# A graph attention kernel: the left sides of its sort by matmul, built in wide VectorE operations or column by column

## The chip, the cores and the metric

One core of a Trainium2 chip runs the kernel in one launch. The time is the device time of that core in microseconds: 1287.59 us is the median of three executions (1286.08, 1287.59 and 4121.88), and the profiled execution took 1285.94 us.

## The reference

A graph layer on 6250 nodes (rows of x, 96 values) and 106,250 edges (src, dst). It computes, cut to what matters:

```
q = (x[src] @ qW), k = (x[dst] @ kW), v = (x[dst] @ vW)      # 4 heads of 24
w = exp(clip(sum over a head of q * k, -10, 10))
res[n] = sum over edges with src = n of (w / (sum of w of the node + 1e-8)) * v
out = layernorm(x + (x + res)), over the 96 values
```

The edges come sorted by dst. The kernel needs them grouped by src, so that a tile of 128 edges has all its sources in one block of 128 nodes.

## The kernel before

**Start.** TensorE projects the nodes; q stays in on-chip memory (`qt`), k and v of all nodes go to a table in device memory (`kv_dram`).

**Sort.** The edges lie as 125 partitions x 850 columns. The columns fall into six groups of 140, 110, 130, 160, 160 and 150. For each group VectorE ranks the edges (`mark`, `pair`, `count`, `base`, `select`, `tree`, `own_position`), which gives every edge its row in a tile (`pos_p`, 0 to 127) and a tile number plus a half (`pos_t`). Then the edges are moved by matmuls, ten columns at a time, called a unit: there are 85 units, 14 of them in group 0. For each column j of a unit TensorE multiplies a left side `lhs[:, q] = (q == pos_p) * payload` (125 partitions x 128) with a right side `theta[:, t]`, a step over the tile numbers, and adds all of a group's products up in `ps_a` and `ps_b`, one for each half of the payload (`pay_a`, `pay_b`). So a unit is 20 matmuls (L620).

- VectorE, `unit`: one comparison over all ten columns at once gives the one-hot tile `lhs_1` (L1037, 125 x 1280 in f16: a ramp `iota_s`, repeated for ten columns, against `pos_p` broadcast over 128 places); two multiplications (L1041, L1044) give `lhs_a` and `lhs_b` with the payloads, broadcast in the same manner. `between(i)` places one of the iteration's own additions (L1103) behind each of the first two.
- ScalarE, `unit`: the steps `theta`, one operation for each column (L707). In group 0 VectorE makes the first four of a unit's ten steps in one operation (L1033, 125 x 744).
- Left and right sides are double buffered by `vm`: a unit waits until TensorE is through with the unit before the last (`s_bin`).

After a group's last unit `differ`, `turn`, `choice` and `pick` turn the sums into the row numbers `dst_s` for the gathers.

**Iterations.** Then 176 iterations of five tiles each: GpSimd gathers the k and v rows of 128 edges with one indirect DMA for each tile (L499, five to a batch, 171 batches, eight buffers); TensorE fetches q by a one-hot matmul (L636), VectorE multiplies q and k (L1122), weighs v (L1132), sums over heads (L1142), adds the results of five tiles to the accumulators (L1103), builds the one-hot tiles of a later iteration (L1111) and clips (L1150); ScalarE takes the exponential and copies; TensorE sums up per node (L650).

**The order** is written out by hand in `plan()`. Group 0 is ranked and sorted before the iterations begin (`sort_stretch`, where VectorE's and the other engines' units run in a loop of two). The ranking and the units of group g (1 to 5) lie within the iterations that use group g-1: first iterations with pieces of the ranking, then iterations with one or two units each; `pick` of group g comes 3 or 4 iterations before the group's first tile. In an iteration VectorE does, in this order, L1122, L1132, an addition, L1142, an addition, L1111, L1150, an addition, and then the unit with the last two additions in it. TensorE does a unit one iteration later than VectorE.

GpSimd issues batch n once VectorE and TensorE are through with a batch some iterations back (6 in the first five groups, 8 buffers in the last), and the first batch of a group once the group is sorted (`s_sorted`, which `pick` signals).

Of the kernel before, what the change touches and what calls it, by code (L numbers as in the profile page):

```python
# [5 lines left out]
def gnn(nc, x, src, dst, qW, kW, vW, out):  # L6
    f32, i32, u16 = mybir.dt.float32, mybir.dt.int32, mybir.dt.uint16
    f16, bf16 = mybir.dt.float16, mybir.dt.bfloat16
    ALU = mybir.AluOpType
    ACT = mybir.ActivationFunctionType  # L10
    AX = mybir.AxisListType

    P = 128
# [6 lines left out]
    EP, EC = 125, E // 125  # L20
# [4 lines left out]
    SU = 10  # L25
    KD = 4
# [4 lines left out]
    GC = [140, 110, 130, 160, 160, 150]  # L31
# [36 lines left out]
    CMAX, TMAX = max(GC), max(TS)  # L68
# [81 lines left out]
    with ExitStack() as ctx:  # L150
        def sb(name, shape, dt):
            return ctx.enter_context(nc.sbuf_tensor(name, shape, dt))
# [4 lines left out]
        def sem(name):  # L157
            return ctx.enter_context(nc.semaphore(name))
# [1 line left out]

        iota_i = sb("iota_i", [P, IW], i32)
        iota_f = sb("iota_f", [P, IW], f32)
        iota_s = sb("iota_s", [P, P, SU], f16)
        pos_h = sb("pos_h", [EP, GC[0]], f16)
        iota_u = sb("iota_u", [P, NB], u16)
        part_i = sb("part_i", [P, 1], i32)
        part_f = sb("part_f", [P, 1], f32)
# [18 lines left out]
        dst_i = sb("dst_i", [EP, EC], i32)  # L186
        tmp_i = sb("tmp_i", [EP, CMAX], i32)
        bin_u = sb("bin_u", [EP, CMAX], u16)
        pay_a = sb("pay_a", [EP, EC], f16)
        pay_b = sb("pay_b", [EP, EC], f16)  # L190
        pos_p = sb("pos_p", [EP, EC], f16)
        pos_t = sb("pos_t", [EP, EC], f32)

        rank_u = sb("rank_u", [EP, CMAX], u16)
        same_u = sb("same_u", [EP, CMAX], u16)
        steps_m = sb("steps_m", [P, max(NB * CMAX, 2 * NPC * PC * D)], f16)
        place_m = sb("place_m", [EP, max(14 * CMAX, 6 * P * SU)], u16)
        kst_m = sb("kst_m", [EP, NB * (KMAX + 2)], f16)
        kb_m = sb("kb_m", [EP, NB * (KMAX + 2)], u16)
        cnt_f = sb("cnt_f", [EP, NB], f32)  # L200
# [29 lines left out]


        LW = P * SU
        lhs_m = place_m[:, 0:6 * LW].bitcast(f16)
        lhs_1 = lhs_m[:, 0:2 * LW].rearrange("p (i q c) -> p i q c", i=2, c=SU)
        lhs_a = lhs_m[:, 2 * LW:4 * LW].rearrange("p (i q c) -> p i q c", i=2, c=SU)
        lhs_b = lhs_m[:, 4 * LW:6 * LW].rearrange("p (i q c) -> p i q c", i=2, c=SU)
        theta = steps_m[0:EP, 0:2 * SU * (TMAX + 1)].rearrange("p (i c t) -> p i c t", i=2, c=SU)
        cum_a = sb("cum_a", [P, max(TMAX + 1, max(GT))], f32)
        cum_b = sb("cum_b", [P, TMAX + 1], f32)
# [9 lines left out]
        ohb = sb("ohb", [P, 4, P, U], bf16)  # L249
        onehT = sb("onehT", [P, 2, U * P], f32)  # L250
        oneh = sb("oneh", [P, 2, U, P], f32)
        T1 = TS[0] + 1
        iota_d = oneh[:, :, :, :].rearrange("p i u n -> p (i u n)").bitcast(f16)[:, 0:T1 * KD]
        iota_d = iota_d.rearrange("p (t c) -> p t c", c=KD)
        theta_d = onehT[0:EP, :, :].rearrange("p i n -> p (i n)").bitcast(f16)[:, 0:2 * T1 * KD]
        theta_d = theta_d.rearrange("p (i t c) -> p i t c", i=2, c=KD)
        prod = sb("prod", [P, 2, U * D], f32)
        score = sb("score", [P, 2, U * HEADS], f32)
        clipped = sb("clipped", [P, 2, U * HEADS], f32)
# [66 lines left out]
        s_lhs_a = sem("s_lhs_a")  # L326
        s_lhs = sem("s_lhs")
        s_half = sem("s_half")
        s_one_lhs = sem("s_one_lhs")
        s_theta = sem("s_theta")  # L330
        s_bin = sem("s_bin")
        s_dif = sem("s_dif")
# [60 lines left out]
        def sort_stretch(eng, unit, g, v0, v1):  # L393

            if not unit:
                return
            a = min(v1, v0 + 2)
            b = a + max(0, v1 - 1 - a) // 2 * 2
            for v in range(v0, a):
                unit(g, v, v % 2)  # L400
            if b > a:
                with eng.Fori(a, b - 1, 2) as i:
                    for k in range(2):
                        unit(g, i + k, (a + k) % 2)
            for v in range(b, v1):
                unit(g, v, v % 2)

        def there(n):
# [105 lines left out]
        def _(pe):  # L514
# [94 lines left out]
            def unit(g, v, vm):  # L609
                w = TS[g] + 1  # L610
                first = isinstance(v, int) and v == V0[g]
                last = isinstance(v, int) and v == V0[g + 1] - 1
                if first:
                    pe.wait_ge(s_blk, g + 1)
                pe.wait_ge(s_theta, v + 1)
                for ps, lhs, s_made in ((ps_a, lhs_a, s_lhs_a), (ps_b, lhs_b, s_lhs)):
                    pe.wait_ge(s_made, v + 1)
                    for j in range(SU):
                        steps = theta_d[:, vm, :, j] if g == 0 and j < KD else theta[:, vm, j, 0:w]
                        mm = nc.tensor.matmul(ps[:, 0:w], lhs[:, vm, :, j], steps,  # L620
                                              start=first and j == 0, stop=last and j == SU - 1)
                    if last and ps is ps_a:
                        mm.then_inc(s_half, 1)
                mm.then_inc(s_bin, 1)

            def tiles(m, mm, sorts):
# [38 lines left out]
                for sort in sorts:  # L665
                    unit(*sort)
# [5 lines left out]
        @block.scalar  # L672
        def _(act):
            act.wait_ge(s_ramp, 1)
            nc.scalar.activation(iota_s[:, :, :], iota_f[:, 0:P].unsqueeze(2).to_broadcast([P, P, SU]), ACT.Copy)
            nc.scalar.activation(iota_d, iota_f[:, 0:T1].unsqueeze(2).to_broadcast([P, T1, KD]), ACT.Copy)
            nc.scalar.activation(iota_t[:, :, :], iota_f[:, 1:P + 1].unsqueeze(2).to_broadcast([P, P, U]),
                                 ACT.Copy).then_inc(s_wide, 1)

# [96 lines left out]
            for j, (a, b) in enumerate(PARTS):  # L776
                act.wait_ge(s_inv, j + 1)
                for i in range(a, min(b, NPC - 1)):
                    for k in range(PC if i < NPC - 2 else HALF):
                        if j + 1 < len(PARTS) and i == b - 1 and k == (PC - 2 if b < NPC - 2 else 2):  # L780
                            root(j + 1)
                        n = i * PC + k
                        last = nc.scalar.activation(yout[i][:, k, :], acc[:, n, 0:D], ACT.Identity,
                                                    scale=inv[:, n:n + 1], bias=shift[:, n:n + 1])
# [4 lines left out]
        def _(dve):  # L789
            own = [0]  # L790

            def link(ins):

                own[0] += 1
                ins.then_inc(s_own, 1)
                dve.wait_ge(s_own, own[0])
# [212 lines left out]
            def own_position(g):  # L1009

                C, _, pl, _, _ = group_views(g)
                c0, c1 = C0[g], C0[g + 1]
                t, s = tmp_i[:, 0:C], src_i[:, c0:c1]
                link(nc.vector.tensor_tensor(t, pl[:, 0, :], rank_u[:, 0:C], ALU.add))
                link(nc.vector.scalar_tensor_tensor(s, t, P - 1, flip[:, 0:C], ALU.bitwise_and, ALU.bitwise_xor))
                link(nc.vector.tensor_copy(pos_p[:, c0:c1], s))
                link(nc.vector.tensor_scalar(t, t, 7, None, ALU.logical_shift_right))
                if g == 0:
                    link(nc.vector.tensor_scalar(pos_h[:, :], t, 0.5, None, ALU.add))
                nc.vector.tensor_scalar(pos_t[:, c0:c1], t, 0.5, None, ALU.add).then_inc(s_pos, 1)  # L1020
                dve.wait_ge(s_pos, g + 1)

            def unit(g, v, vm, between=lambda i: None):
                if isinstance(v, int) and v == 0:
                    dve.wait_ge(s_wide, 1)
                wait(dve, s_bin, v - 1)
                cols = bass.ds(v * SU, SU)

                def spread(a):
                    return a[:, cols].unsqueeze(1).to_broadcast([EP, P, SU])  # L1030

                if g == 0:
                    nc.vector.tensor_tensor(theta_d[:, vm, :, :], iota_d[0:EP, :, :],  # L1033
                                            pos_h[:, cols].unsqueeze(1).to_broadcast([EP, T1, SU])[:, :, 0:KD],
                                            ALU.is_le)
                wait(dve, s_lhs, v - 1)
                nc.vector.tensor_tensor(lhs_1[:, vm, :, :], iota_s[0:EP, :, :], spread(pos_p),  # L1037
                                        ALU.is_equal).then_inc(s_one_lhs, 1)
                between(0)
                dve.wait_ge(s_one_lhs, v + 1)  # L1040
                nc.vector.tensor_tensor(lhs_a[:, vm, :, :], lhs_1[:, vm, :, :], spread(pay_a),  # L1041
                                        ALU.mult).then_inc(s_lhs_a, 1)
                between(1)
                nc.vector.tensor_tensor(lhs_b[:, vm, :, :], lhs_1[:, vm, :, :], spread(pay_b),  # L1044
                                        ALU.mult).then_inc(s_lhs, 1)

            def differ(g):

# [197 lines left out]
            for k in range(HALF, PC):  # L1246
                n = (NPC - 2) * PC + k
                last = nc.vector.tensor_scalar(yout[NPC - 2][:, k, :], acc[:, n, 0:D], inv[:, n:n + 1],
                                               shift[:, n:n + 1], ALU.mult, ALU.add)
            last.then_inc(s_ylast, 1)  # L1250
            n = (NPC - 1) * PC
# [31 lines left out]
```

## Time and profile before

| | |
|---|---|
| median of three runs | 1287.59 us |
| profiled execution | 1285.94 us |
| its span, first to last instruction | 1284.1 us |
| VectorE (DVE) busy | 1030.2 us, 80% |
| TensorE (PE) busy | 988.8 us, 77% |
| GpSimd (POOL) busy | 912.9 us, 71% |
| ScalarE (ACT) busy | 660.6 us, 51% |
| TensorE clock, mean granted | 0.734 |

Busy times are the union of an engine's instructions; instructions of VectorE overlap at their ends, so that the time from start to start of two in a row is shorter than the duration of one. Idle time is put down to what ended it. The clock is given as a share of full speed, 2.4 GHz.

### The profile page before, as it was taken

Reading aid. Unit: us, or ns where it says so; the run is one execution under the profiler, and the core shown is the slowest. Engines: PE = TensorE matmul, PEld = TensorE weight load, DVE = VectorE, ACT = ScalarE, POOL = GpSimd, SP = SyncE. Lnnn points to the kernel's source line nnn. Section 1 sums busy time; section 2 is a strip of 40 time slices with the busy share of each in tenths; the row PEclk is TensorE's granted clock in tenths of the full one; section 3 lists DMA queues with packets and bytes.
Section 4 is the critical chain, followed back from the end, with each engine's and each line's share of the span. In section 5 each row is a group of like instructions: output and inputs, shape, how many; then the busy total and the mean of one; then the engine's idle time right before and its main releaser. Section 6 shows DMA issues by size and latency. Waiting matters only on the chain.

```text
span 1284.1 us, 23009 instructions
## 1 busy us (share of the span) xinstructions
PE 988.8 (77%) x6512; PEld 897.6 (70%) x6513; DVE 1030.2 (80%) x3048; ACT 660.6 (51%) x1469; POOL 912.9 (71%) x887
## 2 busy tenths in 40 slices
PE   8876878678866887867987877878877688888870
PEld 6765776577856887756886766767767677777760
DVE  8999997899889999889987779977768755555557
ACT  6842792259622799223997332587624322222225
POOL 1217787777777777777777777777777777777752
PEclk9986796669875799776898775688859955555555
DMA  6202222222222222222222222222252222222222
GB/s 173 84 13 76 73 66 78 74 69 69 73 79 67 71 71 70 81 75 75 69 69 70 74 73 74 72 71 70 73 150 78 79 80 77 79 78 79 77 62 75
DMA packets 67241, 98.34 MB, mean 77 GB/s; under 512 B 33127, under 2 KB 53204, under 8 KB 67134
## 3 DMA queue, kind: packets, MB, share of 16 engines
q0 software_dynamic: 41040, 84.10, 24.1%
q1 hardware_dynamic: 26094, 12.94, 3.9%
q8 instruction: 51, 0.84, 0.3%
q14 instruction: 56, 0.46, 0.1%
HBM read 89.77 MB, written 7.22 MB: 76 GB/s over the span
## 4 chain that ended last, share of the span: by engine, by line
POOL 27%; DVE 25%; issue 15%; ACT 14%; PE 12%; DVEq 3%; DMA 2%; SPq 0%; POOLq 0%; ACTq 0%
POOL kv L499 27%; ACT steps_m L707 10%; DVE acc L1103 5%; PE ps_r L650 3%; PE ps_q L636 2%; DVE prod L1122 2%; ACT oneh L758 2%; DMA kv<-kv_table,dst_s 2%; DVEq L414 2%; DVE place_m L997 2%; DVE steps_m L834 2%; DVE place_m L1001 2%; PE ps_a L620 1%; ACT onehT L752 1%; PE ps_b L620 1%
## 5 line engine op out<-in xcount | busy, mean ns | idle before, releaser
L499 POOL DMA_INDIRECT kv<-kv_table,dst_s x855 | 890.0, 1041 | 305.3 <-issue 298.9
L636 PE MATMUL ps_q<-qt,onehT 128*128 x1760 | 322.3, 348 | 103.7 <-ACT onehT L752 91.0
L650 PE MATMUL ps_r<-wv,oneh 128*128 128x100 f32 x1752 | 329.9, 356 | 91.7 <-DVE wv L1132 91.4
L636 PEld LDWEIGHTS ps_q<-qt,onehT 128*128 128x128 f32 x1760 | 293.0, 255 | 131.2 <-issue 130.7
L650 PEld LDWEIGHTS ps_r<-wv,oneh 128*128 128x128 f32 x1752 | 301.7, 263 | 109.5 <-DVE wv L1132 105.7
L707 ACT ACTIVATE steps_m<-iota_f,pos_t 125x254 f16<-125x254 f32 (+4 forms) x794 | 311.8, 490 | 17.4 <-PE ps_b L620 10.2
L1103 DVE TENSOR_TENSOR acc<-acc,ps_r 128x100 f32 x876 | 221.2, 252 | 60.2 <-issue 23.7
L1122 DVE TENSOR_TENSOR prod<-ps_q,kv 128x480 f32<-128x480 f32 x176 | 115.0, 653 | 144.1 <-DMA kv<-kv_table,dst_s 138.5
L745 ACT ACTIVATE wv<-clipped 128x20 f32<-128x20 f32 x176 | 38.6, 219 | 360.0 <-DVE clipped L1150 359.8
L752 ACT ACTIVATE onehT<-ps_t 128x640 f32<-128x640 bf16 x176 | 123.7, 703 | 182.6 <-PE ps_t L662 176.6
L758 ACT ACTIVATE oneh<-ohb 128x640 f32<-128x640 bf16 x176 | 163.1, 927 | 1.3 <-PE ps_r L650 1.3
L620 PE MATMUL ps_a<-steps_m,place_m 125*128 125x254 f16 (+4 forms) x794 | 107.7, 287 | 26.8 <-ACT steps_m L707 26.8
L1132 DVE TENSOR_TENSOR wv<-kv,wv 128x480 f32<-128x480 f32 x176 | 114.1, 648 | 2.9 <-issue 2.2
L1142 DVE TENSOR_REDUCE score<-prod 128x20 f32<-128x480 f32 x176 | 113.5, 645 | 0.5
L620 PEld LDWEIGHTS ps_a<-steps_m,place_m 125*128 125x128 f16 x794 | 88.0, 142 | 35.0 <-ACT steps_m L707 29.0
L662 PE MATMUL ps_t<-ident_bf,ohb 128*128 128x128 bf16 x880 | 103.9, 266 | 9.6 <-DVE ohb L1111 9.1
L620 PE MATMUL ps_b<-steps_m,place_m 125*128 125x254 f16 (+4 forms) x794 | 101.8, 277 | 0.0
L662 PEld LDWEIGHTS ps_t<-ident_bf,ohb 128*128 128x128 bf16 x880 | 90.3, 139 | 15.0 <-DVE ohb L1111 13.6
L1111 DVE TENSOR_TENSOR ohb<-iota_t,loc_s 128x640 bf16<-128x640 bf16 x176 | 98.1, 557 | 0.0
L620 PEld LDWEIGHTS ps_b<-steps_m,place_m 125*128 125x128 f16 x794 | 89.7, 141 | 4.1
L1037 DVE TENSOR_TENSOR place_m<-iota_s,pos_p 125x1280 f16<-125x1280 f16 x85 | 69.6, 819 | 6.5 <-PE ps_b L620 6.5
L1041 DVE TENSOR_TENSOR place_m<-place_m,pay_a 125x1280 f16<-125x1280 f16 x85 | 69.6, 819 | 1.6
(204 smaller groups left out, 655.0 us busy)
## 6 DMA issues: line engine op xcount, KB each, us to landing
kv<-kv_table,dst_s POOLq DMA_INDIRECT x855
kv_table<-kv SPq DMA_DIRECT2D x7, 672.0 KB, 3.7
acc<-in_x_dram SPq DMA_DIRECT2D x6, 336.0 KB, 8.1
steps_m<-in_x_dram SPq DMA_DIRECT2D x6, 336.0 KB, 6.6
out_dram<-kv SPq DMA_DIRECT2D x6, 336.0 KB
dst_i<-in_dst_dram SPq DMA_DIRECT2D x1, 415.0 KB
src_i<-in_src_dram SPq DMA_DIRECT2D x1, 346.7 KB
acc<-in_x_dram SPq DMA_DIRECT2D x1, 288.0 KB, 4.5
```

The lines of the kernel that those rows point to most:

```text
L499: nc.gpsimd.indirect_dma_start(kv[:, nm, u, :], None, kv_dram, bass.IndirectOffsetOnAxis(ap=dst_s[:, n * U + u:n * U + u + 1], axis=0)).th ...
L620: mm = nc.tensor.matmul(ps[:, 0:w], lhs[:, vm, :, j], steps, start=first and j == 0, stop=last and j == SU - 1)
L636: last = nc.tensor.matmul(ps_q[nm % 2][:, u * D:(u + 1) * D], onehT[:, nm % 2, u * P:(u + 1) * P], qt[:, bass.ds(blks[u], 1), :].rearrange ...
L650: last = nc.tensor.matmul(to, oneh[:, nm % 2, u, :], wv[:, nm % 2, u, :], start=True, stop=True)
L662: last = nc.tensor.transpose(ps_t[nm % 2][:, u * P // 2:(u + 1) * P // 2].bitcast(bf16), ohb[:, nm % 4, :, u], ident_bf[:, :])
L707: last = nc.scalar.activation(theta[:, vm, j, 0:w], iota_f[0:EP, 0:w], ACT.Sign, scale=-1.0, bias=pos_t[:, bass.ds(v * SU + j, 1)])
L752: nc.scalar.activation(onehT[:, nm % 2, :], ps_t[nm % 2][:, 0:U * P // 2].bitcast(bf16), ACT.Copy).then_inc(s_oneT, 1)
L758: nc.scalar.activation(oneh[:, nm % 2, :, :], ohb[:, nm % 4, :, :].rearrange("p n u -> p u n"), ACT.Copy).then_inc(s_onf, 1)
L1103: nc.vector.tensor_tensor(at, at, from_ps, ALU.add).then_inc(s_acc, 1)
L1122: nc.vector.tensor_tensor(prod[:, nm % 2, :].rearrange("p (u d) -> p u d", u=U), ps_q[nm % 2][:, 0:U * D].rearrange("p (u d) -> p u d", u= ...
L1132: nc.vector.tensor_tensor(wv[:, nm % 2, :, 0:D].rearrange("p u (h d) -> p u h d", h=HEADS), kv[:, km, :, D:2 * D].rearrange("p u (h d) -> ...
L1142: nc.vector.tensor_reduce(score[:, nm % 2, :], prod[:, nm % 2, :].rearrange("p (h d) -> p h d", d=DH), axis=AX.X, op=ALU.add).then_inc(s_s ...
```

## The change

The unit's left sides are made column by column. Each column j of each half is one tensor_scalar of 128 columns: the ramp `iota_h` (f16) is compared with the edge's place `pos_p[:, c]` and multiplied with its payload `pay[:, c]`, both read as one value for each partition. That is 20 operations for a unit where there were three, and `lhs_1` and its semaphore go. `pos_p`, `pay_a` and `pay_b` become f32. The layout of the left sides turns from (place, column) to (column, place), so a matmul reads 128 values in a row. `between(0)` now stands behind the fifth operation and `between(1)` behind the tenth.

In group 0 VectorE's four steps of a unit are four tensor_scalar operations of 186 columns with `pos_t[:, c]` as the scalar, into the same `theta` tile that ScalarE fills; `theta_d`, `iota_d` and `pos_h` go. Units of group 0 are written out one by one on all engines instead of in a loop of two, since a scalar's column is fixed in the instruction.

```
-            nc.scalar.activation(iota_s[:, :, :], iota_f[:, 0:P].unsqueeze(2).to_broadcast([P, P, SU]), ACT.Copy)
-            nc.scalar.activation(iota_d, iota_f[:, 0:T1].unsqueeze(2).to_broadcast([P, T1, KD]), ACT.Copy)
+            nc.scalar.activation(iota_h[:, :], iota_f[:, 0:max(P, TS[0] + 1)], ACT.Copy)
...
-                if g == 0:
-                    link(nc.vector.tensor_scalar(pos_h[:, :], t, 0.5, None, ALU.add))
...
-                        steps = theta_d[:, vm, :, j] if g == 0 and j < KD else theta[:, vm, j, 0:w]
-                        mm = nc.tensor.matmul(ps[:, 0:w], lhs[:, vm, :, j], steps,
+                        mm = nc.tensor.matmul(ps[:, 0:w], lhs[:, vm, j, :], theta[:, vm, j, 0:w],
...
                 if g == 0:
-                    nc.vector.tensor_tensor(theta_d[:, vm, :, :], iota_d[0:EP, :, :],
-                                            pos_h[:, cols].unsqueeze(1).to_broadcast([EP, T1, SU])[:, :, 0:KD],
-                                            ALU.is_le)
-                wait(dve, s_lhs, v - 1)
-                nc.vector.tensor_tensor(lhs_1[:, vm, :, :], iota_s[0:EP, :, :], spread(pos_p),
-                                        ALU.is_equal).then_inc(s_one_lhs, 1)
+                    w = TS[0] + 1
+                    for j in range(KD):
+                        nc.vector.tensor_scalar(theta[:, vm, j, 0:w], iota_h[0:EP, 0:w], pos_t[:, c0 + j:c0 + j + 1],
+                                                None, ALU.is_le)
+
+                def left(to, pay, a, b):
+                    for j in range(a, b):
+                        c = c0 + j
+                        last = nc.vector.tensor_scalar(to[:, vm, j, :], iota_h[0:EP, 0:P], pos_p[:, c:c + 1],
+                                                       pay[:, c:c + 1], ALU.is_equal, ALU.mult)
+                    return last
+
+                left(lhs_a, pay_a, 0, SU // 2)
                 between(0)
-                dve.wait_ge(s_one_lhs, v + 1)
-                nc.vector.tensor_tensor(lhs_a[:, vm, :, :], lhs_1[:, vm, :, :], spread(pay_a),
-                                        ALU.mult).then_inc(s_lhs_a, 1)
+                left(lhs_a, pay_a, SU // 2, SU).then_inc(s_lhs_a, 1)
                 between(1)
-                nc.vector.tensor_tensor(lhs_b[:, vm, :, :], lhs_1[:, vm, :, :], spread(pay_b),
-                                        ALU.mult).then_inc(s_lhs, 1)
+                left(lhs_b, pay_b, 0, SU).then_inc(s_lhs, 1)
```

## Rows read from the trace of the kernel before

**Rows 1.** The page, its first section: busy us (share of the span) xinstructions of each engine.

```profile
PE 988.8 (77%) x6512; PEld 897.6 (70%) x6513; DVE 1030.2 (80%) x3048; ACT 660.6 (51%) x1469; POOL 912.9 (71%) x887
```

**Rows 2.** Timeline, VectorE, an iteration with one unit: start us, us, engine, line, operation.

```profile
429.39 0.64 DVE L1122 TENSOR_TENSOR prod<-ps_q,kv 128x480 f32<-128x480 f32 x1
...
432.14 0.81 DVE L1037 TENSOR_TENSOR place_m<-iota_s,pos_p 125x1280 f16<-125x1280 f16 x1
432.88 0.24 DVE L1103 TENSOR_TENSOR acc<-acc,ps_r 128x100 f32 x1
433.04 0.81 DVE L1041 TENSOR_TENSOR place_m<-place_m,pay_a 125x1280 f16<-125x1280 f16 x1
...
433.95 0.81 DVE L1044 TENSOR_TENSOR place_m<-place_m,pay_b 125x1280 f16<-125x1280 f16 x1
434.68 0.64 DVE L1122 TENSOR_TENSOR prod<-ps_q,kv 128x480 f32<-128x480 f32 x1
```

**Rows 3.** Timeline, VectorE, first operation of the first sort and the one behind it.

```profile
41.63 0.55 DVE L1033 TENSOR_TENSOR onehT<-oneh,pos_h 125x744 f16<-125x744 f16 x1
...
82.98 0.29 DVE L969 TENSOR_SCALAR choice<-iota_f,where 128x138 f16<-128x138 f32 x1
```

**Rows 4.** Windows over the five unit stretches (sum), and VectorE's groups between them and after.

```profile
sum 408.69, PE 347.31 PEld 327.38 DVE 360.18 ACT 364.39 POOL 320.31; mean PE 69.46 PEld 65.48 DVE 72.04 ACT 72.88 POOL 64.06
...
L1122 DVE TENSOR_TENSOR prod<-ps_q,kv 128x480 f32<-128x480 f32 x16 | 10.4, 653 | 8.7 <-DMA kv<-kv_table,dst_s 8.2 <-DVE part L1083 0.2
...
L1122 DVE TENSOR_TENSOR prod<-ps_q,kv 128x480 f32<-128x480 f32 x3 | 2.0, 658 | 9.7 <-DMA kv<-kv_table,dst_s 9.7
```

**Rows 5.** Timeline, VectorE, short operations and the ones behind them.

```profile
3.88 0.26 DVE L811 TENSOR_SCALAR weigh_h<-ones_h,last_p 128x128 f16<-128x128 f16 x1
4.04 0.23 DVE L829 TENSOR_SCALAR tmp_i<-src_i 125x140 int32<-125x140 int32 x1
...
5.11 5.28 DVE L834 TENSOR_SCALAR steps_m<-bin_u 125x140 f16<-125x140 uint16 x49
...
607.96 0.33 DVE L969 TENSOR_SCALAR choice<-iota_f,where 128x208 f16<-128x208 f32 x1
608.20 0.28 DVE L975 TENSOR_SCALAR broken<-iota_f,whose 128x49 f16<-128x49 f32 x1
608.36 0.32 DVE L969 TENSOR_SCALAR choice<-iota_f,where 128x208 f16<-128x208 f32 x1
...
1275.79 0.81 DVE L1248 TENSOR_SCALAR kv<-acc,inv,shift 128x96 f32<-128x96 f32 x3
1276.51 0.85 DVE L1253 TENSOR_TENSOR kv<-acc,inv 128x672 f32<-128x672 f32 x1
```

**Rows 6.** Timeline, GpSimd's gathers and VectorE's operations that they meet.

```profile
432.35 1.43 POOL L499 DMA_INDIRECT kv<-kv_table,dst_s  x1 [0.30 <-issue]
434.08 1.50 POOL L499 DMA_INDIRECT kv<-kv_table,dst_s  x1 [0.30 <-issue]
...
530.29 3.10 DVE L834 TENSOR_SCALAR steps_m<-bin_u 125x160 f16<-125x160 uint16 x24
...
530.91 0.95 POOL L499 DMA_INDIRECT kv<-kv_table,dst_s  x1 [0.30 <-issue]
...
739.09 2.80 DVE L834 TENSOR_SCALAR steps_m<-bin_u 125x150 f16<-125x150 uint16 x25
...
739.27 2.74 POOL L499 DMA_INDIRECT kv<-kv_table,dst_s  x1 [0.31 <-issue]
```

**Rows 7.** Timeline, iteration 122 of VectorE and the last group's first gather.

```profile
945.68 0.66 DVE L1122 TENSOR_TENSOR prod<-ps_q,kv 128x480 f32<-128x480 f32 x1
...
959.48 0.95 POOL L499 DMA_INDIRECT kv<-kv_table,dst_s  x1 [0.30 <-issue]
```

**Rows 8.** Windows of L499 alone: stretch us, GpSimd busy (x gathers), TensorE's clock, DMA share, GB/s.

```profile
609.00:708.00 99.00, 78.27 (x69) 0.90 0.26 70
...
922.40:1243.50 321.10, 244.03 (x254) 0.61 0.32 85
```

More of the change, by code:

```diff
@@ L162, in gnn @@
         iota_f = sb("iota_f", [P, IW], f32)
-        iota_s = sb("iota_s", [P, P, SU], f16)
-        pos_h = sb("pos_h", [EP, GC[0]], f16)
+        iota_h = sb("iota_h", [P, max(P, TS[0] + 1)], f16)
         iota_u = sb("iota_u", [P, NB], u16)
@@ L188, in gnn @@
         bin_u = sb("bin_u", [EP, CMAX], u16)
-        pay_a = sb("pay_a", [EP, EC], f16)
-        pay_b = sb("pay_b", [EP, EC], f16)
-        pos_p = sb("pos_p", [EP, EC], f16)
+        pay_a = sb("pay_a", [EP, EC], f32)
+        pay_b = sb("pay_b", [EP, EC], f32)
+        pos_p = sb("pos_p", [EP, EC], f32)
         pos_t = sb("pos_t", [EP, EC], f32)
@@ L196, in gnn @@
         steps_m = sb("steps_m", [P, max(NB * CMAX, 2 * NPC * PC * D)], f16)
-        place_m = sb("place_m", [EP, max(14 * CMAX, 6 * P * SU)], u16)
+        place_m = sb("place_m", [EP, max(14 * CMAX, 4 * P * SU)], u16)
         kst_m = sb("kst_m", [EP, NB * (KMAX + 2)], f16)
@@ L232, in gnn @@
         LW = P * SU
[L233 to L236, printed above, removed]
+        lhs_m = place_m[:, 0:4 * LW].bitcast(f16)
+        lhs_a = lhs_m[:, 0:2 * LW].rearrange("p (i c q) -> p i c q", i=2, c=SU)
+        lhs_b = lhs_m[:, 2 * LW:4 * LW].rearrange("p (i c q) -> p i c q", i=2, c=SU)
         theta = steps_m[0:EP, 0:2 * SU * (TMAX + 1)].rearrange("p (i c t) -> p i c t", i=2, c=SU)
@@ L251, in gnn @@
         oneh = sb("oneh", [P, 2, U, P], f32)
[L252 to L256, printed above, removed]
         prod = sb("prod", [P, 2, U * D], f32)
@@ L328, in gnn @@
         s_half = sem("s_half")
-        s_one_lhs = sem("s_one_lhs")
         s_theta = sem("s_theta")
@@ L396, in sort_stretch @@
                 return
[L397 to L405, printed above, removed]
+            for v in range(v0, v1):
                 unit(g, v, v % 2)
@@ L1025, in unit @@
                     dve.wait_ge(s_wide, 1)
+                c0 = v * SU
                 wait(dve, s_bin, v - 1)
-                cols = bass.ds(v * SU, SU)
-                def spread(a):
-                    return a[:, cols].unsqueeze(1).to_broadcast([EP, P, SU])
                 if g == 0:
-                    nc.vector.tensor_tensor(theta_d[:, vm, :, :], iota_d[0:EP, :, :],
-                                            pos_h[:, cols].unsqueeze(1).to_broadcast([EP, T1, SU])[:, :, 0:KD],
-                                            ALU.is_le)
-                wait(dve, s_lhs, v - 1)
-                nc.vector.tensor_tensor(lhs_1[:, vm, :, :], iota_s[0:EP, :, :], spread(pos_p),
-                                        ALU.is_equal).then_inc(s_one_lhs, 1)
+                    w = TS[0] + 1
[9 more added lines that the diff above has]
+                left(lhs_a, pay_a, 0, SU // 2)
                 between(0)
-                dve.wait_ge(s_one_lhs, v + 1)
-                nc.vector.tensor_tensor(lhs_a[:, vm, :, :], lhs_1[:, vm, :, :], spread(pay_a),
-                                        ALU.mult).then_inc(s_lhs_a, 1)
+                left(lhs_a, pay_a, SU // 2, SU).then_inc(s_lhs_a, 1)
                 between(1)
-                nc.vector.tensor_tensor(lhs_b[:, vm, :, :], lhs_1[:, vm, :, :], spread(pay_b),
-                                        ALU.mult).then_inc(s_lhs, 1)
+                left(lhs_b, pay_b, 0, SU).then_inc(s_lhs, 1)
             def differ(g):
```

## The prediction

> **What bounds the kernel now.** The page first: VectorE is busy 80% of the span, TensorE 77% and GpSimd 71% [rows 1]. Neither share says who sets the end, so I went to the stretches. After a start of 89 us (ranking and first sort) 176 iterations run; VectorE works through them in a fixed order, and GpSimd issues 171 batches of five row gathers a few iterations ahead. In the timeline of an iteration that carries one sort unit, VectorE goes from one product (L1122) to the next in 5.29 us with no idle time, and each of the unit's three operations (L1037, L1041, L1044) occupies 0.73 to 0.74 us from its start to the next start [rows 2]. So a unit is 2.21 us of VectorE, and what an iteration needs beside it is 3.08. In the first sort nothing else runs on VectorE: 14 units take 82.98 - 41.63 = 41.35 us, 2.95 each, the theta operation L1033 included [rows 3].
>
> Gathers: GpSimd has no gap but 0.30 us between two gathers, so the gather chain runs as a second rope beside VectorE's. In the five stretches with units (64 iterations, 57 with one unit and 7 with two, 71 units) VectorE is busy 360.2 of 408.7 us [rows 4]; most of its idle time there is in the last two, where it waits for gathers. After the last unit it waits for gathers in almost every iteration. Both ropes are nearly taut now; the one that gets longer will set the time.
>
> **The change, part by part.** It removes three wide tensor_tensor operations (125x1280) per unit and puts 20 tensor_scalar operations of 128 columns in their place, each with two per-partition scalars. I need the pitch of one, start to start, since the durations overlap. No row has exactly this form, so I step towards it [rows 5]:
> - scalars in the instruction, 16-bit, 140 columns (L834): 49 in 5.28 us, the last one's end of 0.09 not counted, 0.106 us each;
> - one per-partition scalar, f32 source: 208 columns (L969) 608.20 - 607.96 = 0.24, 49 columns (L975) 608.36 - 608.20 = 0.16, so 0.5 ns a column;
> - one per-partition scalar, 16-bit, 128 columns (L811): 4.04 - 3.88 = 0.16;
> - two per-partition scalars, f32, 96 columns (L1248): three in 1276.51 - 1275.79 = 0.72, 0.24 each.
> L834 and L811 differ by the scalar read, some 0.055 us; L1248 has one scalar more and is 0.08 us longer than L811, though it has fewer columns. I read it as 0.06 us for each scalar over a fixed 0.07, and the columns cheap. The 96 f32 columns of L1248 are 0.051 us at L969's rate; 128 16-bit columns are half that rate, 0.033 (L811 with 128 of them is as short as L975 with 49 in f32). So I take 0.24 - 0.051 + 0.033 = 0.22 us, 0.223 with the third figure kept. The operation is nearly all fixed cost. While gathers run, the operations of L834 take 0.126 us (24 in 3.10 less an end of 0.08 [rows 6]), where 20 more columns explain 0.005 of the 0.020 more; L811 in the quiet start and L975 among gathers show no such surcharge. I take 0.23. Bounds: 0.106 below (scalars free), 0.25 above.
>
> First sort: a unit is 20 x 0.223 = 4.46 plus four theta operations of 186 columns with one scalar, 0.175 each (0.16 and the extra columns), 5.16 in all. 14 x 5.16 = 72.2, against 41.35; the pos_h operation goes (0.27). **+30.7 us**, all on the path, since the gathers cannot start before the first group is sorted. TensorE and ScalarE need under 3 us for such a unit and stay covered.
>
> The five stretches: VectorE needs 64 x 3.08 + 71 x 4.60 = 523.7 us without a wait, against 408.7 now: **+115.0**. Its idle 48.5 us are in the 408.7 and so are already used as cover. Outside them VectorE waits for gathers 8.2 us in one and 9.7 in the other (2.1 of it belongs to the last stretch) [rows 4]; a VectorE that is late does not wait: **-15.8**. So the multiply of iteration 122, behind the last group's pick, comes 30.7 + 115.0 - 15.8 = 129.9 us later than 945.68 [rows 7], at 1075.6.
>
> The end: the last group's 45 batches need that pick and then run at 6.3 us a batch whatever VectorE does. Now the first of them starts at 959.48 [rows 7], 13.8 us after the pick, because GpSimd was behind. After the change GpSimd has been waiting for VectorE (it may be five to eight batches ahead) and starts at once, 2 us for the batch in hand: 1077.6, **+118.1 us**. The tail is unchanged.
>
> What costs nothing: the gathers' own relief. A gather takes 1.13 us on average in the unit stretch shown and 0.96 behind the sorts [rows 8], because some that start under a unit operation last 1.43 or 1.50 instead of 0.95 [rows 6]. That is 69 x 0.17 = 12 us for 16 units, 53 for all. The change takes the long operations away, but the gain goes to a queue that no longer sets the time; if VectorE's cost were small it would be the gain (rivals). ScalarE's narrower ramps at the start save 2 us behind loads that end later: nothing. The unrolled loop: the later groups are written out already and run without idle time; nothing. Contiguous weight columns for TensorE: its unit matmuls hide their loads; only the strided theta of group 0 gets faster, beside a VectorE of 5.16 us.
>
> A rule that speaks for the change: the Trainium skill, "VectorE: DVE Perf Modes", section "The TRN2 errata", gives 58 cycles plus the columns over the mode's factor; for 128 16-bit columns at four a cycle that is 94 ns, an estimate of 1.9 us a unit, faster than now. For L834 it gives 97 ns and the trace has 106; for L1248 it gives 110 and the trace has 240, so the rule as it stands leaves out what scalars from memory cost. The same section advises tiles of 512 elements or more, which speaks against the change, as the rows do.
>
> Sum against the profiled execution: 1285.9 + 118.1 = **1404 us**. That execution is 0.1% below the median of 1287.6; 2% of it, 26 us, is about what a measurement of this kernel tells from no change.
>
> **Rivals.**
> (a) The second scalar costs nothing and L1248 was slow because its columns cost twice L969's rate. Then the pitch is 0.24 - 0.10 + 0.033 = 0.173, 0.18 under gathers: first sort 14 x 4.16 = 58.2, +16.6; stretches 64 x 3.08 + 71 x 3.6 = 452.7, +44.0; -15.8, -13.8, +2: +33, 1319 us. For it: L1248 alone has two scalars, so no row separates its rate from them. Against: the first scalar costs 0.055 by two rows, and L1248's types are those of L969's source. 0.12.
> (b) Both scalars for the price of one, 0.16 and 0.167: +13.0, 197.1 + 237.1 gives +25.5, -15.8, -11.8: +11, 1297 us, no change that can be told. 0.05.
> (c) Faster: scalars are read under the operation before, pitch 0.106 (0.12 under gathers). A unit is 2.4 us, VectorE gets 71 x 0.2 = 14 us longer, the first sort stays, and the gather rope loses 53 us: about -39, 1247 us. It decides from a pitch below some 0.15 us. For it: L834. Against: the two rows with scalars. 0.05. The page's 94 ns would give this case too, some 15 us lower.
> (d) Trains of short operations shut gathers out. One gather that started in a train of L834 lasted 2.74 us instead of 0.95, to the end of the train; another, in a like train, took 0.95 [rows 6]. If each unit holds two gathers up by 1.8 us, an iteration with a unit costs GpSimd 6.3 + 3.6 = 9.9 us against VectorE's 7.7; over 64 iterations 140 us, of which GpSimd wins back some 1 us in each of the 55 iterations between: about 1490 us. 0.05. The Trainium skill, "SBUF — State Buffer", section "Who interferes with whom", says that a VectorE operation in a two-port mode blocks GpSimd wholly and tensor_tensor does not block descriptor writing; for wide tensor_tensor operations this trace shows the contrary, and for short fast ones mostly no delay.
> (e) TensorE is granted 0.90 in the unit stretch and 0.61 behind the sorts [rows 8]. It is busy 347 us in the 64 iterations [rows 4], 5.4 each. Waiting more for VectorE it could fall to the lower level and need up to twice that where VectorE needs 7.7: 1450 to 1500 us. Against: a TensorE without gaps was granted nearly full speed here. 0.05.
>
> **Numbers.** My case has 0.68: 1375 (pitch 0.21) to 1440 (pitch 0.25: 14 x 5.7 gives +38, stretches +143, -27.6, so +153). With (a) the range is 1308 to 1445, which leaves out (b) to (e), 0.20. The likeliest case alone: 1375 to 1445. Faster by over 2%: 0.05. Within 2%: 0.08, (b) and the low edge of (a). Slower: 0.87.
>
> **What would show it.** The pitch of the new operations: 20 in 4.5 to 4.7 us. Iterations with a unit at 7.7 us without VectorE idle time, units of the first sort at 5.2, the first gather at 120, the multiply behind the last pick near 1075, gathers at 0.95 to 1.05 us with GpSimd waiting between batches, no gather wait on VectorE before that pick. I am wrong if the pitch is below 0.17, if VectorE waits for gathers inside the unit stretches, or if TensorE has no gaps there.

## The result and the profile after

The changed kernel takes 1388.75 us (median of four runs, 1388.01 to 1390.07) against 1286.84 us for the kernel before beside it: 1.080 times as long (interval 1.077 to 1.082). The profiled execution has a span of 1388.3 us. Slower was forecast, and by the mechanism named; 1404 was 15 us longer than measured.

The page of the changed kernel, its first section (columns as in [rows 1]), then the shares of the chain that ended last (DVEq is VectorE's instruction sequencer, "issue" is time for which the profile names no wait), then the two groups of new operations (busy us, mean ns of one, idle us ahead of them).

```profile
PE 1015.1 (73%) x6512; PEld 895.0 (64%) x6513; DVE 1221.0 (88%) x4534; ACT 667.4 (48%) x1468; POOL 873.1 (63%) x887
...
DVE 59%; issue 13%; POOL 11%; PE 10%; DVEq 4%; ACT 2%; DMA 0%; ACTq 0%; POOLq 0%; SPq 0%
...
L1017 DVE TENSOR_SCALAR place_m<-iota_h,pos_p,pay_a 125x128 f16<-125x128 f16 x850 | 208.6, 331 | 0.0
L1017 DVE TENSOR_SCALAR place_m<-iota_h,pos_p,pay_b 125x128 f16<-125x128 f16 x850 | 198.8, 318 | 0.0
```

The same chain of the kernel before, where VectorE and GpSimd had about equal parts:

```profile
POOL 27%; DVE 25%; issue 15%; ACT 14%; PE 12%; DVEq 3%; DMA 2%; SPq 0%; POOLq 0%; ACTq 0%
```

VectorE has 190.8 us more of busy time, GpSimd 39.8 less: the gathers got cheaper, and the time still rose. The mean of 318 to 331 ns is not the price of one operation, since neighbours overlap. For that, the timeline of one iteration with a unit, VectorE (answers to [rows 2]):

```profile
738.14 0.64 DVE L1102 TENSOR_TENSOR prod<-ps_q,kv 128x480 f32<-128x480 f32 x1
...
740.89 1.19 DVE L1017 TENSOR_SCALAR place_m<-iota_h,pos_p,pay_a 125x128 f16<-125x128 f16 x5
742.00 0.24 DVE L1083 TENSOR_TENSOR acc<-acc,ps_r 128x100 f32 x1
742.17 1.19 DVE L1017 TENSOR_SCALAR place_m<-iota_h,pos_p,pay_a 125x128 f16<-125x128 f16 x5
743.29 0.24 DVE L1083 TENSOR_TENSOR acc<-acc,ps_r 128x100 f32 x1
743.46 2.31 DVE L1017 TENSOR_SCALAR place_m<-iota_h,pos_p,pay_b 125x128 f16<-125x128 f16 x10
745.70 0.64 DVE L1102 TENSOR_TENSOR prod<-ps_q,kv 128x480 f32<-128x480 f32 x1
```

Five take 742.00 - 740.89 = 1.11 us, ten take 2.24: 0.222 to 0.224 us each, start to start. The iteration is 7.56 us instead of 5.29. Three gathers of GpSimd in that iteration, which start under these operations (answers to [rows 6]):

```profile
741.54 0.94 POOL L483 DMA_INDIRECT kv<-kv_table,dst_s  x1 [1.35 <-issue]
742.79 0.95 POOL L483 DMA_INDIRECT kv<-kv_table,dst_s  x1 [0.30 <-issue]
744.05 0.98 POOL L483 DMA_INDIRECT kv<-kv_table,dst_s  x1 [0.30 <-issue]
```

The sum over the same five stretches with units, with one of them as a row of its own (start:end, length, then PE, PEld, DVE, ACT, POOL busy, granted clock, DMA share, GB/s); answers to [rows 4]:

```profile
707.83:829.08 121.25, 93.90 (x701) 82.24 (x700) 121.25 (x481) 90.93 (x206) 82.03 (x83) 0.85 0.25 68
...
sum 517.13, PE 392.57 PEld 347.02 DVE 516.90 ACT 383.60 POOL 331.49; mean PE 78.51 PEld 69.40 DVE 103.38 ACT 76.72 POOL 66.30
```

VectorE is busy 516.9 of 517.1 us there; before it was 360.2 of 408.7. The group of the multiply between 135.47 and 1061.26 us has no gather among its releasers any more:

```profile
L1102 DVE TENSOR_TENSOR prod<-ps_q,kv 128x480 f32<-128x480 f32 x123 | 79.5, 647 | 2.5 <-PE ps_q L619 1.4
```

The timeline at the marks of [rows 3] and [rows 7]: first operation of the first sort and the one behind it, first gather, iteration 122's multiply, the last group's first gather, the last gather of all (which started at 1242.88 before, and the first one at 89.44).

```profile
42.31 0.80 DVE L1011 TENSOR_SCALAR steps_m<-iota_h,pos_t 125x186 f16<-125x186 f16 x4
...
119.04 0.28 DVE L951 TENSOR_SCALAR choice<-iota_f,where 128x138 f16<-128x138 f32 x1
...
125.71 1.22 POOL L483 DMA_INDIRECT kv<-kv_table,dst_s  x1 [76.87 <-issue]
...
1061.26 0.66 DVE L1102 TENSOR_TENSOR prod<-ps_q,kv 128x480 f32<-128x480 f32 x1
...
1063.60 1.27 POOL L483 DMA_INDIRECT kv<-kv_table,dst_s  x1 [0.30 <-issue]
...
1347.37 0.94 POOL L483 DMA_INDIRECT kv<-kv_table,dst_s  x1 [0.30 <-issue]
```

| step | predicted | measured | from |
|---|---|---|---|
| start, to the first gather | +30.7 | +36.3 | 125.71 - 89.44 |
| five stretches | +115.0 | +108.4 | 517.13 - 408.69 |
| outside them, to iteration 122 | -15.8 | -29.1 | remainder of 1061.26 - 945.68 = +115.6 |
| from there to the last gather | -11.8 | -11.1 | (1347.37 - 1061.26) - (1242.88 - 945.68) |
| sum | +118.1 | +104.5 | |

### The profile page after: what moved, and what is told of

Its sections match the earlier page's. It is cut to its first block, busy times and chain, and to the rows that moved or that the text cites. A ratio compares the mean times of both kernels' runs of the same rounds, so it can differ in the third digit from the quotient of the medians.

```text
span 1388.3 us, 24260 instructions
## 1 busy us (share of the span) xinstructions
PE 1015.1 (73%) x6512; PEld 895.0 (64%) x6513; DVE 1221.0 (88%) x4534; ACT 667.4 (48%) x1468; POOL 873.1 (63%) x887
## 4 chain that ended last, share of the span: by engine, by line
DVE 59%; issue 13%; POOL 11%; PE 10%; DVEq 4%; ACT 2%; DMA 0%; ACTq 0%; POOLq 0%; SPq 0%
DVE place_m L1017 24%; POOL kv L483 11%; DVE acc L1083 8%; DVE prod L1102 4%; DVE wv L1112 3%; PE ps_r L633 3%; DVEq L398 3%; PE ps_q L619 3%; DVE place_m L979 2%; DVE steps_m L816 2%; DVE place_m L983 2%; DVE clipped L1130 1%; DVE ohb L1091 1%; DVE score L1122 1%; DVEq L1083 1%
## 5 line engine op out<-in xcount | busy, mean ns | idle before, releaser
L483 POOL DMA_INDIRECT kv<-kv_table,dst_s x855 | 850.9, 995 | 448.5 <-issue 433.7
L633 PE MATMUL ps_r<-wv,oneh 128*128 128x100 f32 x1752 | 334.1, 358 | 166.2 <-DVE wv L1112 165.7
L619 PE MATMUL ps_q<-qt,onehT 128*128 x1760 | 310.5, 339 | 100.8 <-ACT onehT L734 85.7
L619 PEld LDWEIGHTS ps_q<-qt,onehT 128*128 128x128 f32 x1760 | 283.1, 247 | 126.0 <-issue 125.4
L1017 DVE TENSOR_SCALAR place_m<-iota_h,pos_p,pay_a 125x128 f16<-125x128 f16 x850 | 208.6, 331 | 0.0
L1017 DVE TENSOR_SCALAR place_m<-iota_h,pos_p,pay_b 125x128 f16<-125x128 f16 x850 | 198.8, 318 | 0.0
L603 PE MATMUL ps_a<-steps_m,place_m 125*128 125x254 f16 (+4 forms) x850 | 130.3, 315 | 34.1 <-DVE place_m L1017 23.4
L603 PEld LDWEIGHTS ps_a<-steps_m,place_m 125*128 125x128 f16 x850 | 95.1, 118 | 54.1 <-issue 28.0
L603 PE MATMUL ps_b<-steps_m,place_m 125*128 125x254 f16 (+4 forms) x850 | 120.4, 300 | 9.3 <-DVE place_m L1017 9.0
L603 PEld LDWEIGHTS ps_b<-steps_m,place_m 125*128 125x128 f16 x850 | 94.4, 114 | 26.5 <-DVE place_m L1017 14.7
L645 PEld LDWEIGHTS ps_t<-ident_bf,ohb 128*128 128x128 bf16 x880 | 90.9, 141 | 15.1 <-DVE ohb L1091 13.2
```

What stands on the lines that cost most here:

```text
L483: nc.gpsimd.indirect_dma_start(kv[:, nm, u, :], None, kv_dram, bass.IndirectOffsetOnAxis(ap=dst_s[:, n * U + u:n * U + u + 1], axis=0)).th ...
L603: mm = nc.tensor.matmul(ps[:, 0:w], lhs[:, vm, j, :], theta[:, vm, j, 0:w], start=first and j == 0, stop=last and j == SU - 1)
L619: last = nc.tensor.matmul(ps_q[nm % 2][:, u * D:(u + 1) * D], onehT[:, nm % 2, u * P:(u + 1) * P], qt[:, bass.ds(blks[u], 1), :].rearrange ...
L633: last = nc.tensor.matmul(to, oneh[:, nm % 2, u, :], wv[:, nm % 2, u, :], start=True, stop=True)
L645: last = nc.tensor.transpose(ps_t[nm % 2][:, u * P // 2:(u + 1) * P // 2].bitcast(bf16), ohb[:, nm % 4, :, u], ident_bf[:, :])
L1017: last = nc.vector.tensor_scalar(to[:, vm, j, :], iota_h[0:EP, 0:P], pos_p[:, c:c + 1], pay[:, c:c + 1], ALU.is_equal, ALU.mult)
```

## The experiments

Two questions: is the 0.222 us made of fixed cost, columns or scalars, and where in the program does the time arise? My theory was the one of the prediction (0.06 us for each scalar read); the rivals were that the columns or the mere count of operations cost it, and that the end is set by something else than VectorE.

In e0 to e3b the payloads, and in e1 to e2b the scalars named below, are constants, so the sort yields zeros; its instructions all remain. On two of the chips (that of e0 to e3 and that of e1b to e3b and e8) even the kernel before took 1535 and 1565 us, and the traces of these runs have idle stretches of up to 30 us whose releaser they cannot name. So something there adds some 250 us that the change has nothing to do with. From those runs I use lengths within iterations that have no idle time; the ratios of these runs don't carry over to the 1287 us kernel. The times expected for e0 to e3 and e1b to e3b were for a chip on which the kernel before takes 1287 us, and no run of e0 to e3b tests them. Taken as ratios, e0 came out lower than expected (1.047, not 1.079), and all of e1 to e3b higher, e1 and e1b most clearly (1.012 and 1.009, where 0.97 to 0.98 was expected).

**e0, the payload's scalar from a tile of zeros** (control for the three after it).

```
-  pay[:, c:c + 1], ALU.is_equal, ALU.mult)
+  pay_z[:, c:c + 1], ALU.is_equal, ALU.mult)
```

> The changed kernel with the payload scalar read from a tile of zeros; places and everything else as before, so the sort gives zeros and its output is no result. It is the control for the next three runs: all theories say that the values don't matter, a pitch of 0.223 us for the new operations and 1389 us (1385 to 1393).

Timeline of a unit of the first sort, VectorE:

```profile
52.08 4.55 DVE L1019 TENSOR_SCALAR place_m<-iota_h,pos_p,pay_z 125x128 f16<-125x128 f16 x20
56.52 0.64 DVE L1013 TENSOR_SCALAR steps_m<-iota_h,pos_t 125x186 f16<-125x186 f16 x3
```

(56.52 - 52.08) / 20 = 0.222 us, as in the changed kernel. Ratio to before 1.047 (1.039 to 1.055); iterations with a unit and no idle time last 7.53 to 7.62 us (7.54 to 7.65 in the changed kernel). To the length of an operation and of an iteration the data make no difference, so for these the control serves; for the whole time it can't be said from this chip.

**e1, no scalar from memory.**

```
-  iota_h[0:EP, 0:P], pos_p[:, c:c + 1],
-  pay[:, c:c + 1], ALU.is_equal, ALU.mult)
+  iota_h[0:EP, 0:P], 5.0, 0.0,
+  ALU.is_equal, ALU.mult)
```

> As the control, but both scalars stand in the instruction and none is read from memory (the sort gives zeros). Theory A, each scalar read from memory costs 0.06 us over a fixed 0.07: pitch 0.106, a unit 2.1 us, an iteration with a unit 5.2 us, the gathers become the bound and last 0.95 to 1.0 us each: 1245 to 1260 us, below the kernel before. Rival B, twenty short operations cost 0.22 us each whatever their scalars: 1389 us. Rival C, cheap short operations follow each other so closely that gathers are shut out: pitch 0.11, but gathers of 1.5 us and more in the unit stretches, 1300 us or more.

```profile
50.97 2.13 DVE L1019 TENSOR_SCALAR place_m<-iota_h 125x128 f16<-125x128 f16 x20
53.01 0.81 DVE L1013 TENSOR_SCALAR steps_m<-iota_h,pos_t 125x186 f16<-125x186 f16 x4
```

0.102 us each. Ratio 1.012 (1.003 to 1.020).

**e2, one scalar from memory** (`pos_p[:, c:c + 1], 0.0`).

> As the control, but the payload stands in the instruction, the place is still read (the sort gives zeros). Theory A: pitch 0.16, a unit 3.2 us, an iteration with a unit 6.3 us, which is about a gather batch: first sort 17 us and the units 87 us shorter than in the changed kernel, some of it lost to the gathers, 1285 to 1305 us. Rival B: 1389 us. Rival D, only the second scalar costs: pitch 0.11 and 1250 us.

```profile
51.12 3.33 DVE L1019 TENSOR_SCALAR place_m<-iota_h,pos_p 125x128 f16<-125x128 f16 x20
54.37 0.80 DVE L1013 TENSOR_SCALAR steps_m<-iota_h,pos_t 125x186 f16<-125x186 f16 x4
```

0.1625 us each; ratio 1.042 (1.034 to 1.050). So none, one and two scalars are 0.102, 0.1625 and 0.222: 0.060 us for each, and the second costs what the first does.

**e3, two columns in one operation** (half as many operations, twice as wide, two scalars each; all 20 columns are written, with scalars that fit only one of a pair).

```
-  for j in range(a, b):
+  for j in range(a, b, 2):
...
-      last = nc.vector.tensor_scalar(to[:, vm, j, :], iota_h[0:EP, 0:P], pos_p[:, c:c + 1],
+      last = nc.vector.tensor_scalar(to[:, vm, j:j + 2, :], iota_2[0:EP, :, :], pos_p[:, c:c + 1],
```

> As the control, but each operation covers 256 columns, two of a unit's ten, with one pair of scalars read from memory, so 10 operations for a unit where there were 20 and as many columns in all (the sort gives zeros). Theory A: 0.19 fixed and 0.066 for the columns, pitch 0.257, a unit 2.6 us, an iteration 5.65 us: 1262 to 1280 us. A theory in which the columns carry the cost (0.223 for 128, so 0.446 for 256): a unit still 4.46 us, 1389 us.

```profile
49.17 2.65 DVE L1021 TENSOR_SCALAR place_m<-iota,pos_p,pay_z 125x256 f16<-125x256 f16 x10
51.73 0.80 DVE L1015 TENSOR_SCALAR steps_m<-iota_h,pos_t 125x186 f16<-125x186 f16 x4
```

0.256 us for 256 columns: 128 more cost 0.034, under a sixth of the 0.222. Ratio 1.015 (1.004 to 1.026).

**e4, the clearing of acc on ScalarE.** It tests the cause of the changed kernel's late start: a copy and a memset of 4.18 us on GpSimd coincide with one operation of the first unit that lasts 4.96 us instead of 0.3, and the two operations begun behind it end only with it.

```
-  pool.wait_ge(s_prj, NB)
-  nc.gpsimd.memset(acc[:, :, :], 0.0).then_inc(s_acc0, 1)
...
+  if g == 0 and v == 2:
+      act.wait_ge(s_prj, NB)
+      nc.scalar.activation(acc[:, :, :], iota_f[:, 0:RW].unsqueeze(1).to_broadcast([P, NB, RW]),
+                           ACT.Copy, scale=0.0).then_inc(s_acc0, 1)
```

> The changed kernel with the clearing of the accumulators (4900 columns) on ScalarE ahead of the third unit instead of on GpSimd in the first. Theory A: the one operation of 4.96 us in the first unit was shut out by GpSimd's copy and memset (43.97 to 48.84 us), so all operations last about 0.3 us, the first gather comes 4.3 us earlier and the kernel takes 1384.5 us. Rival: VectorE waited for its instructions when it entered the unrolled code: the stall stays, 1389 us.

The changed kernel, timeline of GpSimd and VectorE:

```profile
43.92 5.00 DVE L1017 TENSOR_SCALAR place_m<-iota_h,pos_p,pay_a 125x128 f16<-125x128 f16 x2
43.97 0.75 POOL L464 COPY qt<-kv 128x672 f32<-128x672 f32 x1 [2.65 <-ACT kv L676]
44.66 4.18 POOL L469 MEMSET acc<- 128x4900 f32 x1
```

e4, VectorE in the same stretch, and its first gather:

```profile
42.16 2.84 DVE L1019 TENSOR_SCALAR place_m<-iota_h,pos_p,pay_a 125x128 f16<-125x128 f16 x10
44.93 2.31 DVE L1019 TENSOR_SCALAR place_m<-iota_h,pos_p,pay_b 125x128 f16<-125x128 f16 x10
47.16 0.79 DVE L1013 TENSOR_SCALAR steps_m<-iota_h,pos_t 125x186 f16<-125x186 f16 x4
...
121.12 1.23 POOL L481 DMA_INDIRECT kv<-kv_table,dst_s  x1 [77.27 <-issue]
```

The stall is gone (no operation over 0.84 us) and gathers start 4.6 us earlier. The rival, that VectorE waited for its instructions, falls. The whole time is 1387.17 us (1386.06 to 1391.23; ratio 1.077, 1.074 to 1.081), where 1384.5 was expected; that is 1.6 us less than the changed kernel, with intervals that overlap: the cause of the late start is shown, its worth in the end time is not resolved.

**e5 and e6, the change in the first sort alone and in the iterations alone** (the kernel before with `columns(g)` choosing between both forms; e5's first sort is written out as in the change). **e7, the kernel before with the first sort's units written out** and nothing else.

```
+  def columns(g):
+      return g == 0        # e6: g > 0
...
-  a = min(v1, v0 + 2)
-  b = a + max(0, v1 - 1 - a) // 2 * 2
+  a = b = v1               # e5 and e7
```

> Columns one by one in the first sort only; the units within the iterations are the wide ones of the kernel before. My account: the first gather comes 36 us later, and since both the gathers and VectorE run without a gap from there, all of it reaches the end: 1287 + 36 = 1323 us. Rival, the iterations make up for a late start: under 1305 us.

> Columns one by one in the units within the iterations only; the first sort is the wide one of the kernel before. My account: VectorE is longer by 108 us in the unit stretches, loses 29 us of waits outside them and 11 at the end: 1287 + 68 = 1355 us, which with the run on the first sort adds up to the whole change. Rival, the late start is what hurts: 1310 us or less.

> The kernel before with nothing changed but that the units of the first sort are written out instead of looped. My account: nothing, 1287 us within 1 us. Rival, entering written-out code costs VectorE some 4 us: 1291 us.

| | us | ratio | interval | first gather |
|---|---|---|---|---|
| e5 | 1321.48 | 1.026 | 1.021 to 1.030 | 126.00 |
| e6 | 1355.11 | 1.052 | 1.048 to 1.057 | 89.02 |
| e7 | 1287.06 | 1.000 | 0.997 to 1.002 | 87.51 |

All three came out as expected. The first sort is worth 35 us, the iterations 69, together 104 against 102 for the whole: the parts add up, so both lie on one chain of work. The traces agree: the five stretches take 409.0 us in e5, as before, and 518.5 in e6. Writing out the loop costs nothing; in its profile the first gather even starts 1.9 us earlier (87.51 against 89.44), which the whole time does not resolve.

**e1b, e2b, e3b: e1 to e3 once more, on another chip, and e8: the kernel before with only lhs_b built by columns, in the last group** (`half_b(g)` is `g == 5`). This is the chip where the kernel before took 1565 us.

> The run without a scalar read once more, for its time on a chip where the kernel before takes 1287 us; the first time it took 1535 there. Its pitch in the first sort was 0.102 us. Theory A: VectorE is no longer the longer rope, the gathers are, and they keep the 50 us that the wide operations cost them: 1245 to 1260 us. Rival C (gathers shut out by close short operations): 1300 us or more.

> The run with one scalar read once more, for its time; its pitch was 0.163 us. Theory A: 1285 to 1305 us, close to the kernel before.

> The run with 256 columns in each operation once more, for its time; its pitch was 0.256 us, so ten operations take 2.56. Theory A: VectorE's units cost nearly what they did and the gathers lose their delays: 1262 to 1280 us, below the kernel before.

> The kernel before, with only the second half of the payload (L1044) made column by column, and only in the last group, where VectorE waits for gathers 1.9 us in each iteration. It costs VectorE 1.5 us in 15 iterations that have it to spare and saves the gathers what L1044 delays them, some 0.2 us for each unit. My account: 2 to 4 us less than before, 1283 to 1285 us, hardly to be told. Rival, the added VectorE time delays the gathers' releases: 1295 us or more.

The fourth column is the median and range of iterations with one unit and no idle time. The last takes the gathers that begin while a unit operation runs, to 0.01 us; for the kernel before it is 1.459 us and 87 of 97, for the changed one 0.955 and 0 of 244.

| | ratio | interval | iteration with a unit | gathers begun under unit operations: mean us, over 1.2 us |
|---|---|---|---|---|
| e1 | 1.012 | 1.003 to 1.020 | 5.20 (5.13 to 5.46) | 1.020, 10 of 103 |
| e1b | 1.009 | 1.006 to 1.012 | 5.15 (5.12 to 5.34) | 1.136, 26 of 92 |
| e2b | 1.026 | 1.022 to 1.031 | 6.37 (6.33 to 6.46) | 0.957, 1 of 123 |
| e3b | 1.012 | 1.007 to 1.016 | 5.65 (5.64 to 5.77) | 0.971, 2 of 120 |
| e8 | 1.004 | 1.001 to 1.008 | wide units | wide units |

e1b, one of its iterations on VectorE, and on GpSimd the longest gather begun under unit operations:

```profile
162.63 0.64 DVE L1104 TENSOR_TENSOR prod<-ps_q,kv 128x480 f32<-128x480 f32 x1
...
166.73 1.13 DVE L1019 TENSOR_SCALAR place_m<-iota_h 125x128 f16<-125x128 f16 x10
167.78 0.64 DVE L1104 TENSOR_TENSOR prod<-ps_q,kv 128x480 f32<-128x480 f32 x1
...
605.49 1.92 POOL L484 DMA_INDIRECT kv<-kv_table,dst_s  x1 [6.86 <-issue]
```

An iteration of 5.15 us is 0.14 shorter than before's 5.29, and the kernel was still not faster. What VectorE waited for in e1b stands at the unit operations (idle us ahead of them, times):

```profile
  remote: 108.9, 19
  PE ps_b L604: 28.1, 5
```

"remote" is a releaser that the trace does not name. The program has only one wait there (but for the very first unit), for TensorE to be through with the unit before the last. e8, whose first unit operation is the wide comparison, has 86.2 and 11.4 us at the same place. And TensorE has idle time on this chip for which the profile names no wait: 155 us in e1b and 125 in e8, where the kernel before has 7 in its profile. Part of it lies between matmuls of one group, as here in e1b, timeline of TensorE:

```profile
814.60 0.25 PE L634 MATMUL ps_r<-wv,oneh 128*128 128x100 f32 x1 [0.15 <-issue]
815.34 0.34 PE L634 MATMUL ps_r<-wv,oneh 128*128 128x100 f32 x1 [0.49 <-issue]
816.76 0.55 PE L634 MATMUL ps_r<-wv,oneh 128*128 128x100 f32 x2 [1.08 <-issue]
818.18 0.33 PE L634 MATMUL ps_r<-wv,oneh 128*128 128x100 f32 x1 [0.88 <-issue]
```

So by the program's order VectorE waited there for TensorE, and the time of e1b doesn't price the short operations. What holds TensorE up on this chip is not known. e8 was expected to be 2 to 4 us faster, and its ratio of 1.004 shows no gain. Whether a unit in cheap short operations beats the wide form on a chip where the kernel before takes 1287 us stays open.

## Why the prediction came out as it did

**The pitch, right.** Predicted 0.223 us from four rows of other operations; measured 0.222. The split holds too: 0.060 us a scalar, 0.034 for 128 columns, and what is left, 0.102 - 0.034 = 0.068, is the fixed part (0.07 predicted), if columns cost without scalars what they cost with two, which no run separates. The prediction had stepped there from 96 columns in f32 at another operation's rate; that step was not tested by itself. Rivals (a), (b) and (c) fall with it: the second scalar costs as much as the first (e2), neither is free (e1). The Trainium skill, "VectorE: DVE Perf Modes", section "The TRN2 errata", gives an estimate of 94 ns for this operation: right within a tenth for e1 (102 ns), which reads no scalar from memory, and 128 ns too low for the changed kernel. The section's rule on a fixed cost for each instruction agrees with the trace; the scalars' share is not in it.

**The first sort, mechanism right, 5.6 us short.** Units take 5.18 us (predicted 5.16), by the chain of first theta operations:

```profile
51.76 0.79 DVE L1011 TENSOR_SCALAR steps_m<-iota_h,pos_t 125x186 f16<-125x186 f16 x4
56.94 0.79 DVE L1011 TENSOR_SCALAR steps_m<-iota_h,pos_t 125x186 f16<-125x186 f16 x4
```

The first unit took 51.76 - 42.31 = 9.45, that is 4.3 more: a VectorE operation lasted until GpSimd's copy and memset had ended, and e4 took that away. I had not looked at what GpSimd does beside the first unit. Another 0.7 is the sort's own later start (42.31 against 41.63).

**The stretches, right, 6.6 us too long.** I took 0.23 under gathers, from L834's operations of [rows 6]. The unit operations show no such surcharge: 0.222 to 0.224. Over 1420 of them, less 0.007 each is 9.9 us; an iteration's remainder of 3.12 us instead of 3.08 (7.56 less 20 x 0.222) gives 2.6 of that back. This surcharge was the mis-sized term. The 6.6 us too many here and the 5.6 too few in the first sort nearly cancel, by luck; the 13.6 us that the sum is off come almost wholly from the next step.

**Outside the stretches, 13.3 us more given back than the 15.8 predicted.** The 15.8 were VectorE's waits for gathers, and they are gone: behind the fourth and the fifth stretch, where all of them were, the iterations take 15.1 us less. The rest I had not listed. Behind the first three stretches, where VectorE had waited for no gather, the iterations take 14.1 us less, and VectorE's idle time there falls from 37.1 us to 24.6: right behind a group's last unit it had waited for TensorE's and ScalarE's share of that unit. Groups of the difference operation, iterations of before and then of after:

```profile
L1054 DVE TENSOR_TENSOR dif<-cum_b 128x253 f16<-128x253 f32 (+3 forms) x5 | 2.0, 403 | 2.8 <-ACT cum_b L730 2.8
L1054 DVE TENSOR_TENSOR dif<-cum_a 128x253 f16<-128x253 f32 (+3 forms) x5 | 2.0, 402 | 3.9 <-ACT cum_a L728 3.9
```

```profile
L1034 DVE TENSOR_TENSOR dif<-cum_b 128x253 f16<-128x253 f32 (+3 forms) x5 | 2.0, 397 | 0.0
```

Those two show 6.7 us of it; the iterations that hold them got shorter by 2 to 4 us each (one from 8.37 to 4.20). My reading is that a slower VectorE lets TensorE finish the unit beside it. e5 and e6 bear it out: outside the stretches and up to iteration 122, e6 is 30.5 us shorter than before and e5, whose units there are the wide ones, 2.2. I had used as cover only the waits for gathers; every wait of the bounding engine is cover.

**The end, right.** From iteration 122 to the last gather 11.1 us less (11.8 predicted); the last group's first gather starts 2.3 us after the pick (2 predicted), where it was 13.8.

**The gathers' relief, right and worth nothing here.** A gather takes 0.988 us in the stretch shown (82.03 / 83) against 1.13 before [rows 8]; summed over all, what gathers take beyond 0.945 us fell from 82 to 43. GpSimd's idle time ahead of gathers grew from 305 to 449 us, and up to iteration 122 no multiply waited for a gather. Rival (d) is false for this kernel: 244 gathers start under the new operations, mean 0.955, the longest 1.09. Where the same trains read no scalars it is true in a small part: 26 of 92 gathers last over 1.2 us in e1b and 10 of 103 in e1. It does not explain why e1b brought no gain: all gathers together take 55 us beyond 0.945 there, less than the 82 of the kernel before, and VectorE's waits stood elsewhere, as shown above. Rival (e) did not come: TensorE was granted 0.78 to 0.86 in the stretches (0.87 to 0.92 before), was busy 392.6 us instead of 347.3, and stayed under VectorE's 516.9.

No sign of being wrong came: the pitch is not below 0.17 us, VectorE waits for no gather in the stretches, and TensorE is idle there for 125 of 517 us. The likeliest case was the one that happened: 104 us more, in the lower half of its own range (1375 to 1445), because waits that vanish were not counted, and a surcharge was that is not there.

## What to carry to other kernels

Count a short VectorE operation by its start-to-start time and by its operands: here a per-partition scalar from memory cost nearly twice what 128 columns of 16 bits did, and 20 small operations with two scalars each took twice as long as the three wide ones (4.46 us a unit against 2.21), although the wide form makes an additional pass. Relief for the engine that is not late (here the gathers, 39 us) does not pay for it. When the bounding engine gets slower, subtract all its waits, not only those for the rival chain of work, and look at what other engines do beside its first operations.

## What the runs showed of the hardware

- A scalar operand from memory: 0.060 us each on a VectorE tensor_scalar of 128 columns (0.102, 0.1625, 0.222 us for none, one, two); 128 further f16 columns 0.034.
- VectorE and GpSimd: a short VectorE operation was held 4.96 us, until GpSimd's copy and memset ended; with the memset on ScalarE (e4) it was not. The Trainium skill, "SBUF — State Buffer", section "Who interferes with whom", says that whichever of the two starts first holds the shared ports and the other fully blocks. The full block agrees; the order doesn't show, since in the trace the held operation begins 0.05 us ahead of GpSimd's copy.
- In the other direction the outcome depends on the operands. Gathers begun under 125x1280 tensor_tensor operations took 1.46 us on average (97 of them, 50 us in sum beyond the 0.95 of an undisturbed one). The prediction calls that contrary to the section just named. It need not be: that section also says that a VectorE instruction with two inputs in on-chip memory contends with a GpSimd instruction that reads there, and a gather has its row numbers `dst_s` there. Under tensor_scalar operations with two scalars from memory a gather took 0.955 (244); under those without 1.020 in e1 and 1.136 in e1b, the longest 1.92. That short operations with scalar reads let the gathers through between them is a reading of these numbers; it was not shown by itself.
